# A graph network's first layer normalises the rows it reads itself, and every second message tile is summed by TensorE

## The reference

```python
x = x + _L1_gnn_ref(_layernorm(x, axis=-1), edge_index, edge_weight1, ...)

def _gine_layer(x, src, dst, edge_attr, eps, We, be, W1, b1, gamma, beta, W2, b2):
    e = edge_attr @ We + be
    m = jax.nn.relu(x[src] + e)
    agg = jax.ops.segment_sum(m, dst, num_segments=x.shape[0])
    h = ((1.0 + eps) * x + agg) @ W1 + b1
    mu = jnp.mean(h, axis=0)
    var = jnp.mean(jnp.square(h - mu), axis=0)
    h = (h - mu) * jax.lax.rsqrt(var + BN_EPS) * gamma + beta
    h = jax.nn.relu(h)
    return jax.nn.relu(h @ W2 + b2)
...
def _layernorm(x, axis=-1, eps=1e-05):
    m = jnp.mean(x, axis=axis, keepdims=True)
    v = jnp.var(x, axis=axis, keepdims=True)
    return (x - m) / jnp.sqrt(v + eps)
```

## Time and profile before

| | us |
|---|---|
| median of 3 runs | 5082.73 (5079.81 to 5098.71) |
| the profiled execution | 5089.71 |
| its span, first to last instruction | 5087.8 |
| TensorE, busy | 4280.2 (84%) |
| VectorE, busy | 2971.1 (58%) |
| ScalarE, busy | 1977.8 (39%) |
| GpSimd, busy | 1244.1 (24%) |

### The profile page before, as it was taken

How to read it: one execution, slowest core, us unless ns; L and a number is a source line. 1 busy time by engine, 2 the same in 40 slices (tenths; PEclk the granted TensorE clock), 3 DMA queues, 4 the chain that set the end, 5 groups by cost and what they waited for, 6 DMA issues and landing times. The chain is left out here.

```text
span 5087.8 us, 66969 instructions
## 1 busy us (share of the span) xinstructions
PE 4280.2 (84%) x22721; PEld 3458.8 (68%) x22721; DVE 2971.1 (58%) x6272; ACT 1977.8 (39%) x3360; POOL 1244.1 (24%) x1188
## 2 busy tenths in 40 slices
PE   7859979699997728850898988989889898898967
PEld 4438868587786616640598866988569884897855
DVE  5557734476786666538555445554455445556877
ACT  1212223222345503310433754347533575334556
POOL 2431123111440016753332013310233103230010
PEclk9979989899998856655699986999779996899965
DMA  9972257521998716759753246532555226554676
GB/s 352 400 256 75 73 195 249 186 76 65 373 406 288 238 41 123 132 100 340 227 162 109 95 155 198 162 101 94 183 181 162 89 92 219 163 161 122 185 182 186
DMA packets 509568, 915.22 MB, mean 180 GB/s; under 512 B 104859, under 2 KB 145419, under 8 KB 508515
## 3 DMA queue, kind: packets, MB, share of 16 engines
q1 hardware_dynamic: 318335, 552.97, 32.1%
q0 software_dynamic: 110592, 227.24, 16.4%
q10 hardware_dynamic: 80376, 131.59, 7.4%
HBM read 587.92 MB, written 322.46 MB: 179 GB/s over the span
## 5 line engine op out<-in xcount | busy, mean ns | idle before, releaser
L706 PE MATMUL hidden_O<-hidden_xh,layer_hi 128*128 128x256 f32 (+1 forms) x2560 | 729.7, 285 | 0.1
L707 PE MATMUL hidden_O<-hidden_xh,layer_lo 128*128 128x256 f32 (+1 forms) x2560 | 717.8, 280 | 0.0
L708 PE MATMUL hidden_O<-hidden_xl,layer_hi 128*128 128x256 f32 (+1 forms) x2560 | 717.7, 280 | 0.0
L706 PE MATMUL output_O<-layer_hi,output_hh 128*128 128x512 f32 (+1 forms) x1268 | 504.2, 398 | 58.1 <-DVE output_hl L1992 42.8
L1871 POOL DMA_INDIRECT hidden_agg<-edge_sums,edge_where x316 | 339.9, 1076 | 757.3 <-DVE hidden_xin L1918 605.8
L1902 ACT ACTIVATE hT<-hidden_O,hidden_b 128x256 f32<-128x256 f32 (+1 forms) x640 | 248.5, 471 | 660.1 <-PE hidden_O L708 660.1
L708 PE MATMUL output_O<-layer_lo,output_hh 128*128 128x512 f32 (+1 forms) x1268 | 503.3, 397 | 0.0
L707 PE MATMUL output_O<-layer_hi,output_hl 128*128 128x512 f32 (+1 forms) x1268 | 503.2, 397 | 0.0
L706 PEld LDWEIGHTS hidden_O<-hidden_xh,layer_hi 128*128 128x128 f32 x2560 | 485.4, 190 | 1.6 <-DVE hidden_xl L1079 1.4
L707 PEld LDWEIGHTS hidden_O<-hidden_xh,layer_lo 128*128 128x128 f32 x2560 | 486.2, 190 | 0.0
L708 PEld LDWEIGHTS hidden_O<-hidden_xl,layer_hi 128*128 128x128 f32 x2560 | 484.5, 189 | 0.0
(11 more groups left out here) (393 smaller groups left out, 9878.4 us busy)
## 6 DMA issues: line engine op xcount, KB each, us to landing
hidden_xin<-g SPq DMA_DIRECT2D x156, 512.0 KB
order_basis<-in_L_gnn_basis SPq DMA_DIRECT2D x48, 1280.0 KB
g<-output_y SPq DMA_DIRECT2D x117, 512.0 KB
edge_sums<-message_res SPq DMA_DIRECT2D x160, 256.0 KB
edge_sums<-relation_res SPq DMA_DIRECT2D x80, 256.0 KB
order_x<-in_x SPq DMA_DIRECT2D x39, 512.0 KB
normed<-order_y ACTq DMA_DIRECT2D x39, 512.0 KB
root_xin<-normed SPq DMA_DIRECT2D x39, 512.0 KB
```

Of the source, the lines that this page charges most:

```text
L706: eng.matmul(out, a_hi, b_hi, start=start, stop=False)
L707: eng.matmul(out, a_lo, b_hi, start=False, stop=False)
L708: return eng.matmul(out, a_hi, b_lo, start=False, stop=stop)
```

## The change

The normalising stage is gone, with the table it wrote. The first layer of the second graph network is written out ahead of the loop (which now runs layers 1 and 2) and reads the rows of `x2`, not yet normalised, with `normal=True`; the other layers have `normal=False`.

In the message stage of the first layer each gathered tile gets row statistics on VectorE, a power on GpSimd (queued three gathers later), a shift on VectorE and the normalising itself on ScalarE, in place; then TensorE adds it to the edge term in PSUM, by a product with the identity matrix in f32. In the other layers this product is made for every second tile (the even ones), with rows as they were gathered, and VectorE adds as before in the odd ones. `X` has four buffers instead of two, and the edge terms are loaded in two parts.

In the hidden stage of the first layer each group gets row statistics on VectorE, the power on GpSimd ahead of its gathers, a shift on VectorE, and the normalising of both tiles on ScalarE ahead of the high part; the mix waits for that. The lists of ScalarE and VectorE are longer by one round, and VectorE's has another order. TensorE's list stays.

```diff
-def norm_phase(core, src, dst, half):
...
@@ message_phase
+    W, R, XR = 4, 8, 4
...
+    summed = lambda t: normal or t % 2 == 0
...
+        sum_of = lambda t: X[t % XR] if summed(t) else z[t // 2 % 2]
...
+                def rstd(t):
+                    eng.wait_ge(s["var"], t + 1)
+                    eng.tensor_tensor(rs[:, t:t + 1], mv[:, t, 1:2], half[:, 0:1], ALU.pow).then_inc(s["rstd"], 1)
+                static_pipeline([(0, gather)] + ([(3, rstd)] if normal else []), ET)
...
                 def add(t):
+                    if summed(t):
+                        return
...
-                static_pipeline([(0, add), (1, low)], ET)
+                if normal:
+                    static_pipeline([(0, stats), (1, shift), (3, low)], ET)
+                else:
+                    static_pipeline([(0, add), (1, low)], ET)
...
+                def norm(t):
+                    eng.wait_ge(s["nb"], t + 1)
+                    eng.activation(x[t % R][:, :], x[t % R][:, :], ACT.Identity, bias=nb[:, t:t + 1], scale=rs[:, t:t + 1]).then_inc(s["nx"], 1)
...
-                static_pipeline([(0, high), (2, result)], ET)
+                if normal:
+                    static_pipeline([(0, norm), (1, high), (3, result)], ET)
+                else:
+                    static_pipeline([(0, high), (2, result)], ET)
...
+                    m = eng.matmul(X[t % XR][:, :], edge_terms[:, t * P:(t + 1) * P], attr_terms[:, :], start=True, stop=not summed(t))
+                    if not summed(t):
+                        m.then_inc(s["E"], 1)
+                        return
+                    if normal:
+                        eng.wait_ge(s["nx"], t + 1)
+                    else:
+                        eng.wait_ge(ga[t % R], (t // R + 1) * 16)
+                    eng.matmul(X[t % XR][:, :], ident[:, :], x[t % R][:, :], start=False, stop=True).then_inc(s["X"], 1)
...
@@ hidden_phase
+                def group(g):
+                    if normal:
+                        rstd(g)
+                    for t, n in tiles_of(last(g)):
+                        gather(g * TILES + t)
...
+                if normal:
+                    static_pipeline([(0, norm), (1, high), (2, evacuate)], NG)
+                else:
+                    static_pipeline([(0, high), (1, evacuate)], NG)
...
                 def mix(g):
-                    eng.wait_ge(ld[g % 2], (g // 2 + 1) * 16)
+                    if normal:
+                        eng.wait_ge(s["nx"], g + 1)
+                    else:
+                        eng.wait_ge(ld[g % 2], (g // 2 + 1) * 16)
...
-                static_pipeline([(0, mix), (1, lambda g: split_lo(eng, s, g, g % 2, last(g), T, xh, xl)), (2, statistics)], NG)
...
+                if normal:
+                    static_pipeline([(1, shift), (0, row_statistics), (2, low), (3, statistics), (1, mix)], NG)
+                else:
+                    static_pipeline([(0, mix), (1, low), (2, statistics)], NG)
...
@@ first_ffn
-    norm_phase(core, rows_out, normed_out, cst.half)
...
@@ second_gnn
+        table = skip if first else g
...
-    with nc.Fori(0, LAYERS - 1) as layer:
-        one_layer(layer, 0)
-    one_layer(LAYERS - 1, 1)
+    one_layer(0, True, False)
+    with nc.Fori(1, LAYERS - 1) as layer:
+        one_layer(layer, False, False)
+    one_layer(LAYERS - 1, False, True)
```

More of the change, by code:

```diff
@@ L1725, in layer_of, with message_phase @@
     return v.rearrange(f"one {names} -> (one {names.split()[0]}) {' '.join(names.split()[1:])}")
-def message_phase(core, ed, table, layer, weight):
+def message_phase(core, ed, table, layer, weight, ident, half, normal):
     nc = core.nc
-    W, R = 4, 8
+    W, R, XR = 4, 8, 4
     CHUNK = 5
-    names = ("w whi wlo terms sel0 sel1 sel2 sel3 sel4 sel5 sel6 sel7 E z mh ml B res zero H hres done st0 st1 st2 st3 swg0 swg1 swg2 swg3 swg4 swg5 swg6 swg7")
+    HEAD = XR * P
+    summed = lambda t: normal or t % 2 == 0
+    of_pe = lambda t: sum(summed(k) for k in range(t + 1))
+    of_dve = lambda t: max(0, t + 1) - of_pe(t)
+    names = ("w whi wlo terms more sel0 sel1 sel2 sel3 sel4 sel5 sel6 sel7 E X z mh ml B res zero H hres done st0 st1 st2 st3 "
+             "bn aggr var rstd nb nx swg0 swg1 swg2 swg3 swg4 swg5 swg6 swg7")
     with core.phase("message", names) as (s, sbuf, psum):
@@ L1739, in message_phase @@
         x = [sbuf(f"x{q}", [P, D]) for q in range(R)]
-        z = [sbuf(f"z{q}", [P, D]) for q in range(W)]
+        z = [sbuf(f"z{q}", [P, D]) for q in range(2)]
         mh = [sbuf(f"mh{q}", [P, D], F32R) for q in range(W)]
@@ L1744, in message_phase @@
         hres = sbuf("hres", [ET, D])
-        X = [psum(f"X{q}", [P, D]) for q in range(2)]
+        bn, mv = sbuf("bn", [P, ET, 6]), sbuf("mv", [P, ET, 2])
+        rs, nb = sbuf("rs", [P, ET]), sbuf("nb", [P, ET])
+        X = [psum(f"X{q}", [P, D]) for q in range(XR)]
         B = [psum(f"B{q}", [P, D]) for q in range(2)]
@@ L1843, in hidden_phase @@
         xin = [sbuf(f"xin{q}", [P, TILES, D]) for q in range(2)]
+        rbn, mv = ([sbuf(f"{n}{q}", [P, TILES, k]) for q in range(W)] for n, k in (("rbn", 6), ("mv", 2)))
+        rs, nb = ([sbuf(f"{n}{q}", [P, TILES]) for q in range(W)] for n in ("rs", "nb"))
         agg = [sbuf(f"agg{i}", [P, D]) for i in range(R)]
@@ L1872, in gather, with rstd @@
                                            bass.IndirectOffsetOnAxis(ap=ed.where[1][0:n, c:c + 1], axis=0)).then_inc(ga[j % R], 16)
-                static_pipeline([(0, gather)], len(tiles))
+                def rstd(g):
+                    wait(eng, s["nx"], g - W + 1)
+                    row_rstd(eng, s, g, mv[g % W], cst.half, rs[g % W], last(g))
+                def group(g):
[3 more added lines that the diff above has]
+                        gather(g * TILES + t)
+                static_pipeline([(0, group)], NG)
             @block.tensor
@@ L1903, in evacuate, with norm, high @@
                     m.then_inc(s["ev"], 1)
+                def norm(g):
+                    eng.wait_ge(s["nb"], g + 1)
+                    for t, n in tiles_of(last(g)):
+                        m = eng.activation(xin[g % 2][0:n, t, :], xin[g % 2][0:n, t, :], ACT.Identity,
+                                           bias=nb[g % W][0:n, t:t + 1], scale=rs[g % W][0:n, t:t + 1])
+                    m.then_inc(s["nx"], 1)
+                def high(g):
+                    split_hi(eng, s, g, g % 2, last(g), T, xh)
                 eng.wait_ge(s["b1"], 16)
-                static_pipeline([(0, lambda g: split_hi(eng, s, g, g % 2, last(g), T, xh)), (1, evacuate)], NG)
+                if normal:
+                    static_pipeline([(0, norm), (1, high), (2, evacuate)], NG)
+                else:
+                    static_pipeline([(0, high), (1, evacuate)], NG)
             @block.vector
@@ L2498, in build @@
         first_gnn(core, cst, ed, a, a["x"], normed0, hidden, x1, normed1, combined)
-        first_ffn(core, cst, a, x1, normed1, probs, x2, g)
+        first_ffn(core, cst, a, x1, normed1, probs, x2)
     x3 = scratch(nc, "x3", (N, D))
```

72 lines of the change are left out of this document (53 added, 19 removed).

## The result

The changed kernel takes 5237.03 us (median of 4 runs, 5227.1 to 5244.39) against 5086.12 us for the kernel before on the same chip: a ratio of 1.0292, 95% interval 1.0265 to 1.0319. It is slower, as forecast. So one or more terms of the sum are wrong.

A forecast was written before the change was run, and what follows sets the result against it. TensorE was taken as the bound, at the low clock in message stages and the high one in the hidden stage. -121.9 + 55 + 44 + 274 = +251 us on 5089.71 gave 5341, median 5334 us; range 5270 to 5387, widened to 5230 to 5420.

The forecast's parts named there:

- Part 1: Normalising stage: it goes, nothing runs beside it, so no cover is lost; -121.9 us.
- Part 4: First hidden stage: TensorE waits 4.6 us a group for the mix and loses 2.5 us to the low clock; +274 us.
- the loads stay ahead: First hidden stage: a group's load has 5.6 us before its row statistics could delay the chain, so no cost.
- Part 2: Three later message stages: the identity product adds 1.14 us in 16 even tiles each, at the low clock; +55 us.
- one more pass: Message stages: an f32 identity product streams 0.42 us longer than a reduced one, two passes in all, 0.85 us.
- 0.29 us for the wait: Message stages: an instruction with a wait costs TensorE about 0.29 us beyond its streaming, counted in the identity product's 1.14 us.
- Rival (e): Message stages: the identity product takes four passes, 0.86 us more in 40 + 48 tiles; +76, 5410 us; chance 0.04.
- Part 3: First message stage: TensorE normalises and sums every tile at 3.01 us a tile, with a later start; +44 us.
- message stages at clock 1.00: Sign against the prediction, which had the later message stages at clock 0.50 with 4.9 us for two tiles.
- Rival (c): Message stages reach the high clock, bound by DMA in later ones, POOL in the first; +124, 5207 us; chance 0.05.
- rival (a): First hidden stage: the gap is there but the clock holds; 175 instead of 274, 5235 us; chance 0.08.
- 38 x 1.5: First hidden stage: lower bound of the clock loss, 3 us at the low clock after each gap; -42 us against the forecast.

The follow-up runs named there:

- run 3: The changed kernel with 36 products that nothing reads ahead of TensorE's wait for each group's mixed rows in the first hidden stage: 5149.73 us.
- run 1: The changed kernel with the mix ahead of the statistics in VectorE's list of the first hidden stage: 5117.55 us, 1.0049 of the kernel before.
- run 5: The changed kernel with the identity product over 256 of the 512 columns in all four layers: 5317.83 us.
- run 4: The changed kernel without the identity product in the three later layers, where VectorE makes every sum again; X keeps four buffers: 5270.25 us.
- run 8: The changed kernel with the identity product in every message tile of the later three layers instead of every second one: 5307.48 us.
- run 6: The kernel before with a useless f32 identity product into a spare bank in every second message tile: 5071.52 us, 0.9964 of the kernel before.

## Why the prediction was right in sign and wrong in size

- **Part 1, right.** 121.9 is a length in the kernel before, and what had to be tested is whether something else fills the place. It does not. The last transfer that the expert stage issues on GpSimd, first before and then after, and the message stage's first:

```profile
2265.76 1.98 POOL L1521 DMA_INDIRECT x<-routed_res,routed_token  x1 [0.30 <-issue]
...
2269.92 1.98 POOL L1521 DMA_INDIRECT x<-routed_res,routed_token  x1 [0.31 <-issue]
...
2284.69 0.27 SPq L1726 DMA_DIRECT2D message_attr_terms<-edge_attr_rows  x1
```

From the end of that instruction to the first load of the next stage it is 2280.53 - 2267.74 = 12.79 us before and 2284.69 - 2271.90 = 12.79 us after. No cover was lost.
- **Part 4, right, in its working too.** 13.6 us a group forecast, 13.67 measured; a gap of 4.6, measured 4.41 idle; 2.5 us lost to the clock, measured 2.47 by run 3. A chain that ran off the path in the trace of before had its later price written on it. One sentence there was incomplete: "the loads stay ahead". They do so only because the stage was so slow; with the mix moved forward (run 1) the load behind the turn became the next wait, some 1.9 us a group.
- **Part 2, wrong: the step "one more pass".** I read the 1.054 us of line 1830 as one product and found it one streaming time longer than a reduced product. But the earlier trace rows counts eight such instructions from 2492.2 to 4337.3, and there are four message stages with one border product each: two instructions a product. The product therefore lasts 2.08 us at the lower clock and adds 1.71 us to a tile, not 1.14; the forecast's price, without its 0.29 us for the wait, is that of half a product (0.86 us, run 5). Those 0.29 us were misread as well: of the two instructions with a wait in the earlier trace rows L1816 takes 0.72 us from start to start, but L1824 only 0.59. Rival (e) had the four passes, with the wait on top. The Trainium skill's page FP8 and Floating Point Precision, section TensorE Precision Notes, has a true FP32 product go through the array four times. The runs here agree: half a product takes 0.86 us, four times the 0.213 us of a reduced one of its shape (run 5).
- **Parts 2 and 3, wrong: the clock was held at 0.50.** I argued that the clock can't rise since products fill 59.3 of 60.0 us already. That share doesn't tell: it stands beside 0.50 there, and 45.57 of 46.00 us stands beside 1.00 in the changed kernel. Runs 4 and 5 and the changed kernel all keep TensorE busy in their later message stages, and of these three only the one with the whole f32 products goes to 1.00. Once it does, the old products of a pair take 2.20 us in place of 3.74, and the new one's 0.84 us is more than paid for. The prediction had named message stages at clock 1.00 as a sign that it is wrong, and in this part it is. Rival (c), with a chance of 0.05, gave -39 for the later stages and +11 for the first; measured were -34.6 and +11.5. Its limits were not quite the right ones: a tile is set by TensorE at its upper clock, 3.04 / 2 = 1.52 us in the later stages, not by DMA at 1.46, and 1.95 us in the first, as in run 8, not by GpSimd at 2.1. And that its sums agree so closely is partly luck: the same first stage took 98 to 121 us in six profiles and the same three later ones were 19 to 35 us shorter than before in four, by the moment at which the clock rose.
- **The sum.** By rival (c) the whole was +124, and +13 us lie in unchanged stages, which makes 137 of the 145.9 measured; what is left is 4 us each in the hidden stage and the later message stages. (e)'s premise and (c)'s outcome came true together; I had priced them as two cases that exclude each other, (e) with the product at the lower clock only. That the time lies in the range at all is luck: its lower end had been moved to 5230 for rival (a), a clock that holds through the gap, and that did not happen (2.47 us a group were lost to it). What brought the time down there is the message stages. One bound is also 4 us off (38 x 1.5 is 38 us less than 38 x 2.5, not 42), which changes nothing.

## What to carry to other kernels

Where a step is moved in a hand-written list, follow the chain that then stands between the end of one group's products and the start of the next; its length can be read off the trace beforehand, even while it costs nothing. A stage added to a pipelined loop needs its place in every engine's list: here the same work cost 278 us or 7 us by order alone. And count instructions against products before a duration is taken as a product's price: a line with twice as many as the loop makes is two of them each. What a product then adds is the difference from start to start between a tile with it and a tile without.

## What the runs showed of the hardware

An f32 product of 128x128 by 128x512 appears as two instructions and adds 1.71 us at the lower clock and about 0.85 at the upper one. Products whose results nobody reads, one in every second message tile, made a kernel 0.36% faster (run 6).

A busy share of 1 stands beside either clock, and the moment of the rise differs from run to run. These are ten microseconds of the first message stage, 37 to 39 us into it, whose program is the same in both kernels: first the changed kernel, whose clock rose 31 us into the stage,

```profile
2324.00:2334.00 10.00, 10.00 (x28) 4.47 (x26) 8.73 (x26) 9.18 (x16) 8.02 (x11) 1.00 0.84 258
```

then run 1, where it rose after 66 us:

```profile
2324.00:2334.00 10.00, 10.00 (x16) 4.04 (x14) 5.08 (x15) 5.41 (x9) 3.96 (x6) 0.50 0.47 153
```

TensorE is busy for all ten in both, with 28 instructions in one and 16 in the other; the stage took 104.2 us in one and 120.5 us in the other. What decides the moment of the rise stays open, and so does why half an identity product (run 5) never brings it. Over the six profiles that have this stage unaltered (the changed kernel and runs 1 to 4 and 8) the rise came 19 to 67 us into it and the stage took 98 to 121 us, while stages that stay at the lower clock (the later ones of run 4) repeat within 2 us.
